# CoPE attention: selection in two row groups, table products behind the logits, the sum ahead of the values, the maximum ahead of the bends

## The reference

```
logits = einsum('bhqd,bhkd->bhqk', Q, K) / sqrt(d)            # 1024 x 1024 a head
gates  = sigmoid(logits)
pos    = min(flip(cumsum(flip(gates))), 63)                   # sum of the gates from key k to the end
table  = einsum('bhqd,dn->bhqn', Q, pos_emb)                  # 64 values a query
cope   = table[ceil(pos)] * w + table[floor(pos)] * (1 - w),  w = pos - floor(pos)
out    = softmax(logits + cope) @ V
```

## Time and profile before

| | us |
|---|---|
| median of 3 runs | 13640.67 (13613.76 to 13658.9) |
| profiled execution | 13691.15 |
| its span | 13689.2 |
| PE busy | 11636.6 |
| DVE busy | 7724.8 |
| POOL busy | 6636.8 |
| ACT busy | 4384.1 |
| mean granted clock of PE | 0.889 |

### The profile page before, as it was taken

The page is one execution under the profiler, slowest core; times in us unless marked ns, Lnnn a source line. Parts: engine busy times, 40 slices in busy tenths (PEclk is TensorE's granted clock), DMA queues, the critical chain, the costliest instruction groups (busy, mean ns, idle before and its releaser), DMA issues. The chain is left out here.

```text
span 13689.2 us, 172386 instructions
## 1 busy us (share of the span) xinstructions
PE 11636.6 (85%) x54902; PEld 7795.5 (57%) x54902; DVE 7724.8 (56%) x14164; ACT 4384.1 (32%) x7378; POOL 6636.8 (48%) x5384
## 2 busy tenths in 40 slices
PE   8777899986688888888888888888888888888745
PEld 3555333334366666666666666666666666666521
DVE  0111444432266676667667766666667666666533
ACT  0011233321133333333333333333333333333210
POOL 0000000000077777777777777777777777777500
PEclk9789999987799999999999999999999999999866
DMA  3111222221111111111111111111111111111123
GB/s 76 47 46 43 74 76 76 76 65 61 58 38 40 42 42 38 39 42 41 40 38 41 42 42 37 40 42 41 40 38 42 41 41 37 40 42 41 36 70 104
DMA packets 1054791, 669.07 MB, mean 49 GB/s; under 512 B 804354, under 2 KB 846082, under 8 KB 1054738
## 3 DMA queue, kind: packets, MB, share of 16 engines
q1 hardware_dynamic: 981010, 659.99, 16.7%
q10 hardware_dynamic: 73728, 8.42, 0.4%
HBM read 482.28 MB, written 185.60 MB: 49 GB/s over the span
## 5 line engine op out<-in xcount | busy, mean ns | idle before, releaser
L1311 POOL TENSOR_TENSOR c_total<-c_total,c_over 128x384 f32<-128x384 f32 (+3 forms) x3584 | 3402.5, 949 | 400.0 <-DVE c_over L1211 123.0
L929 PE MATMUL c_pickps<-c_table,c_hot 128*128 128x112 f32 x16384 | 3311.4, 374 | 267.0 <-DVE c_hot L1180 258.8
L929 PEld LDWEIGHTS c_pickps<-c_table,c_hot 128*128 128x128 f32 x16384 | 3187.7, 223 | 529.8 <-issue 523.4
L1188 DVE COPY_PREDICATED c_pickps<-c_upper,c_pickps 128x256 f32<-128x256 uint32 (+1 forms) x1024 | 798.9, 826 | 2176.3 <-PE c_pickps L929 2176.3
L1278 POOL IOTA c_digitrow<- 1x128 f32 x1 | 0.3, 256 | 3678.7 <-POOLq L66 3678.7
L1311 POOL TENSOR_TENSOR c_total<-c_total,c_middle 128x1024 f32<-128x1024 f32 x512 | 1201.2, 2346 | 990.4 <-DVE c_middle L1202 990.2
L1062 ACT ACTIVATE c_over<-c_place,c_thresholds 128x384 f32<-128x384 f32 (+3 forms) x3584 | 1589.9, 526 | 0.0
L1211 DVE TENSOR_TENSOR c_over<-c_over,c_pickps 128x384 f32<-128x384 f32 (+3 forms) x3584 | 1437.2, 446 | 0.0
L1290 POOL TENSOR_TENSOR c_place<-c_place 128x512 f32<-128x512 f32 x768 | 977.2, 1272 | 774.5 <-ACT c_place L1050 733.0
L1299 POOL TENSOR_TENSOR c_place<-c_place 128x1024 f32<-128x1024 f32 (+1 forms) x512 | 1060.2, 2093 | 427.2 <-DVE c_place L1175 427.2
L947 PE MATMUL c_scoreps<-c_total,c_ident 128*128 128x512 f32 x2048 | 1237.1, 736 | 0.0
(11 more groups left out here) (210 smaller groups left out, 14100.7 us busy)
## 6 DMA issues: line engine op xcount, KB each, us to landing
c_digits<-t_digits SPq DMA_DIRECT2D x512, 256.0 KB
t_tables<-c_tablesb SPq DMA_DIRECT2D x256, 256.0 KB, 2.0
c_table<-t_tables SPq DMA_DIRECT2D x1024, 56.0 KB, 2.3
a_q<-t_qa SPq DMA_DIRECT2D x64, 512.0 KB
a_k<-t_ka SPq DMA_DIRECT2D x64, 512.0 KB
c_kb<-t_kb SPq DMA_DIRECT2D x256, 128.0 KB, 2.3
a_q<-t_qa SPq DMA_DIRECT2D x128, 128.0 KB, 2.4
a_k<-t_ka SPq DMA_DIRECT2D x128, 128.0 KB, 2.5
```

The costliest lines, as they stand in the source:

```text
L929: mm = nc.tensor.matmul(pick_ps[:, h // 4, 0:WIDTH, r * 8:(r + 1) * 8], hot[t % 2][:, h, :], table[s][:, :, :, t * 16 + h].rearrange("p l ...
L1188: ins = nc.vector.copy_predicated(pick_ps[:, :, at:at + width, :], far.unsqueeze(2).to_broadcast([128, 4, width, 32]), pick_ps[:, :, at + ...
L1311: nc.gpsimd.tensor_tensor(a, a, b, ALU.add).then_inc(s_add, 1)
```

## The change

Four things change.

1. The selection is split by rows. Its 16 products of 128 rows become 32 of 64 rows (g = 0, 1), each with 4 of the 8 queries and 56 columns. Consecutive products use the upper and the lower half of the rows in turn, and write to different banks (2g + h // 8). A result's elements now stand 8 apart instead of in runs of 8. For this the anchors and tables are stored in another order of queries: the anchor's store (one DVE instruction of 512 elements, L1167) becomes two, and the copy of a table product (one ACT instruction of 512, L1040) four of 128.
2. The table products of the quad after the next leave slot 3. One stands behind the logits in slot 2, one in the same place in slot 3, and each copy stands first in its slot on ACT. The place sums now wait for the first copy.
3. On PE, the sum stands ahead of the values. `start_at` is no longer added on DVE; PE adds it in the turn of the maximum with a product of its own, which stands ahead of the wait for the maximum and behind the wait for `norm`.
4. On DVE, the maximum stands ahead of the first of the bends (product 2), and the reciprocal behind it.

```diff
             def tables(i, n):
                 if n == 0:
                     pe.wait_ge(s_qka, 32 * (i + 1))
-                    after(pe, s_anchorsb, i)
+                    after(pe, s_gate, 8 * i)
                 else:
                     pe.wait_ge(s_tablesb, 2 * i + 1)
+                    after(pe, s_anchorsb, i)
-            def places(i, s):
+            def places(i, s, kept=None):
                 pe.wait_ge(s_gate, 8 * i + 8)
+                if kept is not None:
+                    pe.wait_ge(s_tablesb, kept)
...
-                    r = h % 4
-                    mm = nc.tensor.matmul(pick_ps[:, h // 4, 0:WIDTH, r * 8:(r + 1) * 8], hot[t % 2][:, h, :],
-                                          table[s][:, :, :, t * 16 + h].rearrange("p l m -> p m l"), start=True, stop=True)
+                    for g in range(2):
+                        rows, lanes = slice(64 * g, 64 * g + 64), slice(4 * g, 4 * g + 4)
+                        mm = nc.tensor.matmul(pick_ps[:, 2 * g + h // 8, 0:WIDTH, h % 8:32:8], hot[t % 2][rows, h, :],
+                                              table[s][rows, lanes, :, t * 16 + h].rearrange("p l m -> p m l"),
+                                              start=True, stop=True)
...
             def turn_peak(n, x):
+                after(pe, s_norm, n)
+                nc.tensor.matmul(soft_ps[:, 0:128], start_at[x][:, :], ident[:, :], start=True, stop=False)
                 pe.wait_ge(s_peak, n + 1)
-                after(pe, s_norm, n)
-                nc.tensor.matmul(soft_ps[:, 0:128], peak[x][:, :], ident[:, :], start=True, stop=True).then_inc(s_peakps, 1)
+                nc.tensor.matmul(soft_ps[:, 0:128], peak[x][:, :], ident[:, :], start=False, stop=True).then_inc(s_peakps, 1)
...
-                elif t == 3 and at in (1, 2) and not final(i, 2):
-                    tables(i + 2, at - 1)
+                elif t > 1 and at == 0 and not final(i, 2):
+                    tables(i + 2, t - 2)
...
                     piece(i, t, 0)
+                    if one:
+                        add_cope(n - 1, 1 - x)
                     if two:
...
                             values(n - 2, x, s)
-                    if one:
-                        add_cope(n - 1, 1 - x)
                     piece(i, t, 1)
...
-                        places(i + 1, 1 - s)
+                        places(i + 1, 1 - s, None if final(i, 2) else 2 * i + 5)
...
+                kept = table_sb[n][:, :].rearrange("p (g l t e h) -> p g l t e h", g=2, l=4, t=4, e=2)
+                made = gate_ps[:, :].rearrange("p (t g e l h) -> p g l t e h", t=4, g=2, e=2, l=4)
+                for g in range(2):
+                    for e in range(2):
+                        ins = nc.scalar.activation(kept[:, g, :, :, e, :], made[:, g, :, :, e, :], ACT.Copy)
+                ins.then_inc(s_tablesb, 1)
...
+                turned = anchor[:, :].rearrange("p (b l e h) -> p b l e h", l=4, e=2, h=8)
+                plain = rounded[:, :].rearrange("p (b e l h) -> p b l e h", l=4, e=2, h=8)
+                for e in range(2):
+                    ins = nc.vector.tensor_scalar(turned[:, :, :, e, :], plain[:, :, :, e, :], EIGHTS, None, ALU.subtract)
+                ins.then_inc(s_anchor, 1)
...
-                nc.vector.tensor_reduce(peak[x][:, :], score_ps[:, :, :].rearrange("p k q -> p q k"), AX.X, ALU.max).then_inc(s_top, 1)
-                dve.wait_ge(s_top, n + 1)
-                nc.vector.tensor_tensor(peak[x][:, :], peak[x][:, :], start_at[x][:, :], ALU.add).then_inc(s_peak, 1)
+                nc.vector.tensor_reduce(peak[x][:, :], score_ps[:, :, :].rearrange("p k q -> p q k"), AX.X, ALU.max).then_inc(s_peak, 1)
...
+                    if one:
+                        top(n - 1, 1 - x)
+                    product(i, s, t, 2)
                     if two:
                         recip(n - 2, x)
-                    product(i, s, t, 2)
-                    if one:
-                        top(n - 1, 1 - x)
```

More of the change, by code:

```diff
@@ L758, in build_cope_attention @@
             sem(f"c_s{n}") for n in ("edge", "anchor", "near", "hot", "muxed", "start", "prod", "peak", "rowmax", "less", "rden"))
-        s_chain, s_placed, s_add, s_held, s_top = (sem(f"c_s{n}") for n in ("chain", "placed", "add", "held", "top"))
+        s_chain, s_placed, s_add, s_held = (sem(f"c_s{n}") for n in ("chain", "placed", "add", "held"))
         block = open_block(nc, ctx, sems)
@@ L1021, in _ @@
             turn_anchor(0)
+            pe.wait_ge(s_anchorsb, 1)
             for n in range(2):
@@ L1039, in keep_table @@
                 after(act, s_tablerows, 32 * i)
-                nc.scalar.activation(table_sb[n][:, :].rearrange("p (l x) -> p l x", l=8), gate_ps[:, :].rearrange("p (x l) -> p l x", l=8),
-                                     ACT.Copy).then_inc(s_tablesb, 1)
+                kept = table_sb[n][:, :].rearrange("p (g l t e h) -> p g l t e h", g=2, l=4, t=4, e=2)
[4 more added lines that the diff above has]
+                ins.then_inc(s_tablesb, 1)
             def gate(i, s, n):
@@ L1087, in aside @@
                             gate(i + 1, 1 - s, 4 * t + at)
-                        elif t == 3 and at in (1, 2) and not final(i, 2):
-                            keep_table(i + 2, at - 1)
+                        elif t > 1 and at == 0 and not final(i, 2):
+                            keep_table(i + 2, t - 2)
                     aside(0)
@@ L1166, in near @@
                 dve.wait_ge(s_edge, 4 * i + 5)
-                nc.vector.tensor_scalar(anchor[:, :].rearrange("p (t l h) -> p t h l", t=4, l=8),
-                                        rounded[:, :].rearrange("p (t h l) -> p t h l", t=4, l=8), EIGHTS, None, ALU.subtract).then_inc(s_anchor, 1)
+                turned = anchor[:, :].rearrange("p (b l e h) -> p b l e h", l=4, e=2, h=8)
[3 more added lines that the diff above has]
+                ins.then_inc(s_anchor, 1)
                 dve.wait_ge(s_anchor, i + 1)
```

## The result

The changed kernel takes 13,867.6 us (median of 4 runs, 13,841.51 to 13,901.75) against 13,641.2 for the kernel before in the same runs: ratio 1.0169, 95% interval 1.0136 to 1.0202. It is 1.7% slower; 12,207 us had been forecast, 12.0% less than what came. Its profiled execution took 13,843.17 us with a span of 13,841.3 and a mean granted clock of 0.816 (before 0.889).

The account below looks back on a forecast made before the run. PE as a single file, with selection and rest both on every slot's path, was taken as the bound. Savings of 2 x 2.8 + 1.8 + 3.8 = 11.2 us a quad, 128 quads, 1434 us, gave 12,207 us; range 11,800 to 12,900.

Parts of the forecast that it names:

- The selection at 3.7 us: PE's selection in each slot, 64 records with two row groups overlapping: 3.7 us, from 6.23.
- The second and third rivals: Selection: no overlap beyond weights or strided writes cancel the gain, 13,330 us, 8%; single-value writes slower, up to 16,560, 6%.
- the rival in which POOL and the clock close up: Whole quad: PE waits more, low-clock time doubles, about 4.5 us a quad, 12,780 us; with POOL nearly full; 14%.
- the argument that the new order breaks up the small work: PE: table product and sum now interrupt the logits and values after which the clock falls; no size given.
- it holds that rate at a low clock too: Old selection into slot 0 took 6.63 us at clock 0.82, against 6.23 in slot 1.
- 10.1 + 3.7: Slots 0 and 1: selection starts at +10.1 us and takes 3.7, so 13.8 a slot from 16.6.
- for the scaling 0.9 in slot 2: Slot 2 on PE: values end at +6.2 us, ACT's scaling at +7.1, before the start values and maximum.
- 1.1 for the anchors: Slot 2: PE waits about 1.1 us ahead of the anchor's turn, which stays at +15.0.
- 2 for the one-hot matrix: Slot 3: PE still idles about 2 us ahead of the selection, waiting for the one-hot matrix.
- the 0.5 for the scaling: PE idles about 0.5 us ahead of the start values' turn, waiting for ACT's scaling.
- 0.1 at most: Slot 2 on DVE: storing the anchor in two pieces costs 0.1 us at most.
- 1.25 allowed: ACT's table copy in slot 2, four of 128 elements: 1.25 us allowed, from 0.60 as one; done by about +4.1.

Follow-up runs that it names:

- The order alone: Changed kernel with the old selection (128 rows, 112 columns) and its old store orders turned back in: 13,557.6 us, ratio 0.9938 to the kernel before.
- The variant with 128-row products: Kernel before with each selection product cut in two of 56 columns, all on 128 rows, no row split: 15,668.2 us, ratio 1.1496.
- the best version: Changed kernel plus unread products (a third ahead of slot 3's selection), earlier reciprocal, output transfer behind gate copy, PE loop over twelve quads: 12,115.1 us, ratio 0.8885.

## Why the prediction was wrong

- **The selection at 3.7 us: right**, 3.74. Also right that the groups overlap and that writes of single values cost nothing visible: 64 records of 56 columns run at 0.058 each, 0.117 a pair. The second and third rivals fall. The Trainium skill's rule on writes that are not contiguous (Advanced Engine Details and Errata, PSUM Cachelines), quoted in the prediction, is not borne out by these writes.
- **The clock: the step that failed.** The forecast priced slots 0 and 1 at the full clock and left slots 2 and 3 little time at the low one. It gave the rival in which POOL and the clock close up 14% and "about 4.5 a quad", 12,780 us. Against it stood the argument that the new order breaks up the small work "after which the clock falls today", and that slots 0 and 1 show 1.00. The order alone does raise the clock (0.93 from 0.91). But how long the clock stays low depends on the selection, and nothing in the sum did: the old one hardly slows at a low clock ("it holds that rate at a low clock too" was in the prediction) and got the clock back by itself in 124 of 368 low stretches; the new one doubles in length and did so in none of 381. Low time went from 12.4 to 29.2 us a quad, where the rival had 20 by its estimate. Filling the waits takes it to 4.2 and gives 10.0 us a quad back (73.22 to 63.25), of the 13.0 by which the forecast was too low. That is 0.40 us for each microsecond of low clock, and the rival's price was 0.45: its price was about right, its amount and its reason were not. It had more falls after more waits; there were 3.0 falls a quad against 2.9, and each lasted more than twice as long. The only rival that made the kernel slower than before was the third, by its writes, and that one fell.
- **Slots 0 and 1, "10.1 + 3.7": the first part was mis-sized**, 10.9. The forecast followed the late scaling to the turn of the start values and stopped there; ACT's copy of the gate stands in the same queue behind it and a transfer. With the reciprocal and the transfer both moved, slot 1 takes 13.9 us, and 13.8 was forecast: 0.75 us. Taken for slot 0 as well, 1.5 a quad.
- **PE's code: not in the prediction at all.** Sixteen more products a slot lengthen the loop's code; the page of before has 27 packets on that queue, and the prediction did not ask what would come with a longer body. 61 stops, 0.9 us a quad by themselves. With the clock restored the effect can be read alone: in the kernel with five unread products slots 0 with a stop take 19.8 us and those without 14.8, so 5.0 for a stop of 2.7 on average, or 2.4 a quad. The Trainium skill, Runtime: NRT & Kernel Launch, Instruction fetch mechanics, says that a taken branch whose target isn't held forces a fetch before execution can go on. The place and the count of the stops agree: 61, 30 and 9 for loops of 62, 31 and 10 turns, none in the first turn, which no branch leads to. That the packets carry the loop's first block is inferred, not shown. The variant with 128-row products has 582 packets and no such stop. A slower selection that leaves time for the fetch would explain it; no run tests that.
- **Slots 2 and 3.** The waits were foreseen (for the scaling 0.9 in slot 2, from its +6.2 to +7.1: 1.20, and 0.60 in slot 3; 1.1 for the anchors: 1.43; 2 for the one-hot matrix: 2.57). In slots 0 and 1 the 0.5 for the scaling did not come, 0.17 in slot 1. The anchors' store in two pieces took 1.33 us, from 0.63, and not "0.1 at most". It can account for the 0.3 us by which the wait for the anchors is longer. ACT's four copies took 0.74 to 0.79 (1.25 allowed) and PE had no wait for them.
- **The sum.** Clock 10.0, stops and what follows them 2.4, gate copy 1.5: 13.9, against 73.2 - 59.4 = 13.8 from after to the best version. That the two agree so closely is in part luck. The parts were measured one behind the other and not all apart; the loop over four quads gave back 0.56 a quad where half of 2.4 would be expected, the early reciprocal with the moved transfer 0.5 where 1.5 would be, and the last run, with its third unread product and its ten turns, the other 2.8.

## What to carry to other kernels

Before halving a group of products, ask what it does at PE's lower clock: the old group of 112 columns hardly slowed down there, the new one, bound by weight loads, took twice as long, and a group that stands right behind a wait may then lose more than the halving gives. A few long products that nothing reads, put in PE's known waits, were worth 9% here with the short products, and 1% with the old ones. When the number of products in a loop grows, look at the instruction queue and for idle time put down to "issue" at the loop's start; more steps per turn made it rarer here.

## What the runs showed of the hardware

- Fp32 products of 56 columns with a weight load each: 0.058 us a record on alternating halves of the rows (3.74 us for 64), 0.113 on all rows; at half clock 0.110 and about 0.21.
- PE busy without a gap at the low clock for 20.48 us, with such products for 9.4 of them and then logits, a gate, values and most of a sum, did not get it raised; in after it rose in a sum of 512-column products after 13.65 us, in before within a selection of 112-column ones after 3.42. 124 of 368 low stretches of before hold only such 112-column products; none of 381 of after holds only 56-column ones.
- In the quad shown the clock fell around idle times of 2.57 us and of 1.43 us. With 0.76 of the 2.57 left, and the others filled too, it stayed up for most of the stage (0.97).
- PE's loop with the longer body stops at each turn but the first, 1.5 to 2.1 us in after and 1.3 to 4.3 in the one with unread products. The code moved falls far less than the turns do (643, 551 and 518 packets, 10.5 to 8.5 MB, for two, four and twelve quads a turn; the last with unread products).
